# Gated cross-attention and a routed feed-forward layer: two weight loads, one share and two TensorE products placed elsewhere

## The reference

```python
x = x + tanh(g_xattn) * attention(layernorm(x), ctx, Wq, Wk, Wv, Wo)
x = x + tanh(g_ffn)   * ffn(layernorm(x), gate_w, gate_up_proj, down_proj)
```

```python
probs = softmax(x @ gate_w.T); w, idx = top_k(probs, 2); w = w / sum(w)
for each expert e:            # I = 1024
    g, u = split(x @ gate_up_proj[e].T)
    acc += combine[:, e] * (silu(g) * u @ down_proj[e].T)
```

## Time and profile before

| what | value |
|---|---|
| time, median of 3 runs | 438.24 us (438.04 to 438.81) |
| time of the profiled execution | 438.3 us |
| its span, first to last instruction | 436.5 us |
| mean granted TensorE clock | 0.969 of full |
| busy: TensorE, VectorE, ScalarE, GpSimd | 400.1, 213.2, 207.7, 255.1 us |
| chain that ended last | TensorE 75%, DMA 7%, GpSimd 5%, VectorE 4%, ScalarE 3%, issue 3% |

### The profile page before, as it was taken

One profiled execution on the slowest core, in us unless ns is written; L12 is line 12 of the kernel. 1 busy time (PEld: TensorE's weight loads), 2 busy tenths in 40 slices (PEclk: granted clock), 3 DMA queues, 4 the chain that ended last, 5 costly groups with the idle time before them and its releaser, 6 DMA issues.

```text
span 436.5 us, 10544 instructions
## 1 busy us (share of the span) xinstructions
PE 400.1 (92%) x2483; PEld 336.3 (77%) x2484; DVE 213.2 (49%) x582; ACT 207.7 (48%) x456; POOL 255.1 (58%) x251
## 2 busy tenths in 40 slices
PE   6979688899899999999999999999999999999960
PEld 6646446567788889888888988888888888888850
DVE  2556888789344544433443443454444344444430
ACT  1569876546633374356347332742356336432310
POOL 3105677794596389539728952595339827953221
PEclk9998889799999999999999999999999999999995
DMA  8970024504455325424612552164124621112211
GB/s 271 403 285 25 26 84 145 188 26 126 134 139 202 49 36 206 130 40 131 206 25 43 198 133 37 25 202 135 25 29 121 202 59 25 25 25 38 38 31 15
DMA packets 19629, 46.71 MB, mean 107 GB/s; under 512 B 2368, under 2 KB 13760, under 8 KB 16512
## 3 DMA queue, kind: packets, MB, share of 16 engines
q1 hardware_dynamic: 11632, 35.18, 23.4%
q0 software_dynamic: 6720, 9.64, 12.3%
q10 hardware_dynamic: 1248, 1.57, 1.0%
HBM read 37.64 MB, written 9.00 MB: 107 GB/s over the span
## 4 chain that ended last, share of the span: by engine, by line
PE 75%; DMA 7%; POOL 5%; DVE 4%; ACT 3%; issue 3%; SPq 0%; POOLq 0%; DVEq 0%; ACTq 0%
PE att L1073 21%; PE sc L1051 20%; PE misc L1051 10%; PE qbank L1051 10%; PE pT L1061 6%; DMA rows_scratch<-x 2%; DMA x<-in_x 2%; POOL dn L491 2%; ACT gu L678 2%; PE att L997 2%; PE att L843 1%; DMA out<-xT_all,index_out 1%; PE qbank L863 1%; PE sc L876 1%; POOL dn L422 1%
## 5 line engine op out<-in xcount | busy, mean ns | idle before, releaser
L567 POOL DMA_INDIRECT out<-xT_all,index_out x34 | 54.5, 1603 | 105.7 <-DVE xT_all L1363 97.1
L1073 PE MATMUL att<-dn,hT 128*128 x816 | 113.8, 289 | 1.5 <-DVE xT_all L1363 1.5
L1073 PEld LDWEIGHTS att<-dn,hT 128*128 128x128 f32 x816 | 101.6, 190 | 1.7 <-issue 1.7
L1051 PE MATMUL sc<-gu,xT 128*128 x408 | 102.1, 399 | 0.0
L1051 PEld LDWEIGHTS sc<-gu,xT 128*128 128x128 f32 x408 | 74.2, 188 | 14.6
L1051 PE MATMUL misc<-gu,xT 128*128 x204 | 80.5, 395 | 2.0 <-issue 1.1
L1051 PE MATMUL qbank<-gu,xT 128*128 x204 | 80.1, 393 | 0.0
L416 POOL TENSOR_TENSOR gu<-wraw,gu 128x2048 f32 (+1 forms) x14 | 64.5, 4626 | 1.6 <-issue 1.5
L1340 DVE TENSOR_TENSOR xT_all<-xT_all,sc 128x512 f32<-128x512 f32 x34 | 23.4, 689 | 83.2 <-ACT xT_all L762 83.2
L762 ACT ACTIVATE xT_all<-misc 128x512 f32<-128x512 f32 x34 | 20.3, 597 | 71.8 <-PE qbank L1051 71.7
L1340 DVE TENSOR_TENSOR xT_all<-xT_all,qbank 128x512 f32<-128x512 f32 x34 | 23.4, 688 | 59.5 <-ACT xT_all L762 59.5
(11 more groups left out here) (202 smaller groups left out, 472.7 us busy)
## 6 DMA issues: line engine op xcount, KB each, us to landing
wraw<-in_gu SPq DMA_DIRECT2D x16, 1024.0 KB, 5.4
wraw<-in_dn SPq DMA_DIRECT2D x8, 1024.0 KB, 5.1
x<-in_x SPq DMA_DIRECT2D x8, 266.0 KB, 12.3
xT_all<-in_xT SPq DMA_DIRECT2D x4, 512.0 KB, 11.6
out<-x SPq DMA_DIRECT2D x8, 256.0 KB, 2.6
rows_scratch<-x SPq DMA_DIRECT2D x3, 532.0 KB, 3.6
xT_all<-rows_scratch,index_in POOLq DMA_INDIRECT x36, 2.9
out<-xT_all,index_out POOLq DMA_INDIRECT x34, 3.9
```

Source lines behind the costliest of these rows:

```text
L567: nc.gpsimd.indirect_dma_start(out=out_d, out_offset=bass.IndirectOffsetOnAxis(ap=index, axis=0), in_=y[:, r, :], in_offset=None, compute_ ...
L1051: mm = nc.tensor.matmul(bank[2 * hf + n][:, :], xT[:, par, xp, k, :], gu_part(where, wp, k * 2 * I + col, HALF), start=(k == 0 and xp == 0 ...
L1073: mm = nc.tensor.matmul(bank[6][:, 0:D], hT[:, hf, hp, j * P:(j + 1) * P], dn_part(where, wp, (hf * JH + j) * D, D), start=(hf == 0 and j ...
```

## The change

Three parts of the hand-written order change; no computation is added to or taken from the result.

1. Pieces 3 and 4 (expert 1's gate and up weights) were loaded in batch 3's and batch 4's turn of the sync queue; both are now loaded in batch 2's, behind that batch's store of `x`. GpSimd raises `w_lo` by 2 in its turn 2 instead of turn 4.
2. On GpSimd, `share_out` of set 2 (batches 4 and 5) stands ahead of `mark_places` of batch 5 and of `last_rstds`, where it stood behind them.
3. On TensorE, turn 7 has two products more, of 512 and of 384 columns, whose results nobody reads: one ahead of `ranks`, one behind the second half of the transposed probabilities. Both wait for `lead_ready`.

```diff
@@ sync engine, loop over b
                 sp.dma_start(out_v[:, TB * b:TB * b + TB, :], x[:, TB * b:TB * b + TB, 0:D]).then_inc(out_init, 16)
-                if 3 <= b <= 4:
-                    load_piece(b)
+                if b == 2:
+                    load_piece(3)
+                    load_piece(4)
@@ GpSimd, loop over t
                 if t == B - 1:
                     place_values(NS - 3)
                     mark_places(B - 4)
+                    share_out(NS - 3)
                     mark_places(B - 3, 0, PICKS // 2)
                     last_rstds()
                     mark_places(B - 3, PICKS // 2)
-                    share_out(NS - 3)
                     share_out(NS - 2)
...
-                if t == 4:
+                if t == 2:
                     pool.wait_ge(w_lo_first, 2 * (PIECE // CHUNK))
                     pool.sem_inc(w_lo, 2)
@@ TensorE
+            def stay_warm(n):
+                pe.wait_ge(lead_ready, 1)
+                nc.tensor.matmul(qbank[:, 0:n], ident, const[:, 0:n], start=True, stop=True)
...
                 if t + 1 < B:
                     scores(t + 1)
+                if t == B - 1:
+                    stay_warm(512)
                 if t < B and t - 2 in ENDS:
                     ranks(ENDS[t - 2])
...
                     transpose_probs(t, 1)
+                if t == B - 1:
+                    stay_warm(384)
```

## The result

| | median | runs |
|---|---|---|
| after | 441.01 us | 4, 440.0 to 441.4 |
| before, same chip | 438.14 us | 4, 437.81 to 438.81 |

The ratio is 1.006, with a 95% interval of 1.0031 to 1.0089: the change makes the kernel 0.6% slower, where 436.3 us was forecast and 437.9 was the upper end. The profiled execution of after took 440.0 us (span 438.2), 1.7 us more than that of before.

The account below looks back on a forecast made before the run. TensorE bounds the block loop, so block 2's start decides: 1.6 us earlier, cut to 1.15 at `h_low(0, 0)`, plus 0.84 us of wait removed, makes 2.0 us, 438.3 to 436.3 us; own range 435.4 to 437.1, widened to 437.9 with rivals.

Parts of the forecast that it names:

- The lead store and the first gather: Sync queue and GpSimd: store lands in 3.6 us instead of 5.98, gather moves to 81.3, 1.6 us earlier.
- The two products: TensorE, turn 7: 0.97 and 0.72 us, covered to within 0.1 us if the clock stays full.
- The clock falls anyway, at the old place: Rival, TensorE after 81.6: second product costs 1.43 us at half clock; 438.7 us, chance 0.11.
- VectorE is then the later one: VectorE, batches 6 and 7: without its wait done at 86.55, block 0's first product 1.6 us earlier.
- TensorE, VectorE and GpSimd all stand 1.6 us earlier: Ahead of block 0: all three engines shift 1.6 us, block 0's first product from 90.05 to 88.45.
- get in each other's way less: VectorE and GpSimd: less mutual hindrance, a reason for the range's lower side, down to 435.4 us.
- The later fall of the clock: Rival, TensorE's stand from about 86.1: half clock 6.8 us, block 2 0.7 later; 439.0 us, chance 0.09.
- GpSimd becomes the bound: Rival: GpSimd's chain stays, the moved share adds 0.62 us, `last_rstds` ends at 98.9; 437.6 us, chance 0.18.
- The share: GpSimd, set 2: 0.62 us ahead of `last_rstds`; earlier row store removes TensorE's 0.84 us wait for block 2's rows.
- The price of the change: Block 2's first product: from 113.13 to 111.15, 2.0 us earlier, giving 436.3 us.

Follow-up runs that it names:

- e2: The kernel before with part 1 alone, weight pieces 3 and 4 loaded in batch 2's turn: 440.11 us, ratio 1.0056.
- e1: The kernel after, with GpSimd waiting for VectorE's slots of batches 4 and 5 before its last three low parts: 437.07 us, ratio 0.9983.
- e9: The kernel after without GpSimd's last three low parts, a plain ScalarE copy in their place (wrong numbers): 435.07 us, ratio 0.9906.
- f1: The kernel after with ScalarE's plain copy for the three low parts and three GpSimd memsets in their place: 439.77 us, ratio 1.0040.
- e4: The kernel before with part 2 alone, set 2's share ahead of batch 5's marks: 437.95 us, ratio 1.0000.
- the hold: Added to the kernel after: GpSimd waits for slots of batches 4 and 5 before its last three low parts; 0.9983 with the products, 0.9977 without.
- VectorE's low parts: The kernel after with the three low parts made by VectorE instead of GpSimd: 436.15 us, 0.9948; without the two products 436.30 us, 0.9958.
- e11: The kernel after without the two products and without GpSimd's three low parts, ScalarE's plain copy in their place: 435.76 us, ratio 0.9931.
- e3: The kernel before with part 3 alone, the two long products: 439.35 us, ratio 1.0042.
- e8: The kernel after with GpSimd's wait for the slots, but pieces 3 and 4 loaded at their old place: 438.74 us, ratio 0.9997.
- e6: The kernel after, with the three low parts waiting until VectorE's slot marks of batches 4 and 5 are done: 439.67 us, ratio 1.0024.
- e5: The kernel after, with GpSimd waiting for each low part's end before starting the next: 440.28 us, ratio 1.0029.

## Why the prediction was wrong, point by point

**The lead store and the first gather: right.** The store's 532 KB landed in 3.4 us (forecast 3.6), the gather stood at 80.97, 1.04 behind the tokens (forecast 81.3 and 1.02). Of the 1.6 us, GpSimd got 1.9.

**The two products: right in themselves.** They took about 0.96 and 0.7 us, both covered, and the clock stayed full from 80 to 90. The rival "The clock falls anyway, at the old place" is out.

**The step that failed** is "VectorE is then the later one. It had no work left at 86.21 - 0.72 = 85.49 … without the wait it is done at 86.55", and what follows from it, "TensorE, VectorE and GpSimd all stand 1.6 us earlier". I moved VectorE's and GpSimd's work by the same amount as if each were alone; where it names their collision at all, it has them "get in each other's way less", on the lower side of the range. But the parts of the change moved them by different amounts: VectorE's `slots` stayed where it was, from the tokens on, and GpSimd's gather and low parts moved 1.9 to 2.2 us towards it. The AND met them at their start and grew from 0.17 to 4.06 us; VectorE was done at 89.79, 3.2 later than forecast. That the loads alone do it is shown by e2, and that GpSimd's work in this place is what does it by e1, e9 and f1. The trace of before had the signs, and I didn't price them: VectorE's step `ties` at 88.44 took 1.06 us where the same step takes 0.18 in after, and ended with GpSimd's low parts.

**The later fall of the clock** was on record at 9%, with 439.0 us. It came, and in the place named, TensorE's stand ahead of batch 7's attention; but it isn't what cost the time. The rival had a stand of 0.9 us, half clock for 6.8 us and block 2 0.7 us later. Measured were a stand of 4.45 us, half clock for 3.4 us (90.1 to 93.5) and block 2 1.75 us later. Block 0 was to start at 88.45 and started at 91.81, and 3.2 of these 3.4 us are the late normalisation. The slow products cost TensorE some 0.7 us more up to 94.2, and nothing of that is left at block 2, which is as late against before as block 0 was. That 439.0 lay nearer to the result than the forecast is luck.

**"GpSimd becomes the bound"** fell in this form: GpSimd's chain was earlier, not later. It was its company that cost.

**The share: half right.** Block 2's gather no longer waits for the row stores but for the tokens; TensorE still waited 0.56 us for the rows, which were 4.66 us under way where I had taken 3.0. Alone the share is worth nothing that the times show (e4). GpSimd's last shares weren't done at about 100.6: the first of the two began at 101.73, after GpSimd had stood for 3.16 us (the profile names no releaser; ScalarE made their `odds` from 101.11), and the second was done at 103.49.

**The price of the change: mis-sized.** With the collision gone the change is worth 435.07 against 435.89, and 436.15 against 437.02: 0.8 and 0.9 us, not the 2.0 of the forecast (the intervals of the two ratios overlap in each pair, so the size is rough). And the products, on which half of the argument rested, give nothing that the times show clearly: 0.9983 with and 0.9977 without them under the hold, 0.9948 and 0.9958 with VectorE's low parts. Only e9 against e11 has 0.7 us, within the 0.5 to 1.5 expected if they are worth something, and there too the intervals overlap.

**What stays open.** The profiled execution of after lost 1.7 us, the medians 2.9; the other executions had no profile. That a run of three low parts holds one VectorE instruction for all three isn't explained. In e3, e4 and e8 too one step waited past the end of at least one low part, up to the end of the last. But in before's turn 4 a run of four, from 43.43 to 48.38, delayed three steps by 0.5 to 0.7 us each and let them go in between, and in e6 the same run of three (84.66 to 88.40) let VectorE in behind its second. And e6's ratio is 0.4% above e1's, while its stretch from the tokens to block 2 is only 0.4 us longer; I have no cause for that.

## What to carry to other kernels

When an edit moves one engine earlier, lay its new timeline beside those of the others instruction by instruction; in this kernel VectorE and GpSimd couldn't be moved past each other for nothing, and an instruction of 0.17 us took 4. Look in the trace of before for instructions whose longest is many times their median (289 and 1056 ns for the line of `ties` at 88.44): if such a one ends with an instruction of another engine, it may be a collision that the kernel already pays for. A stand that holds two engines back may be what keeps two others out of each other's way, so price the removal of a wait with its neighbours' work, not alone.

## What the runs showed of the hardware that I had not expected

A VectorE instruction on 128x8 integers waited for GpSimd for up to 3.9 us. The wait ended with the last of three low parts made back to back (87.27 and 87.23), and with pauses between them after the first (1.62 us in e5). The instruction's recorded start was 0.26 us ahead of the run's, while GpSimd issued a gather; in before the same instruction took 0.17 us during a gather alone. The wait was as long behind memsets (3.85 us in f1) as behind subtractions. Two-input steps of VectorE waited behind the subtractions as well (3.59 us in e3, 3.39 for the two of e5), and GpSimd's own run grew by 1.0 us in e1. Reductions didn't: one at 86.02 in e6, in the middle of a low part, took 0.17.

The Trainium skill, "SBUF — State Buffer", section "Who interferes with whom", says that VectorE and GpSimd share one pair of ports with an exclusive lock, that a `tensor_scalar` or a copy in a two-port mode contends for it, that an instruction with two inputs in the scratchpad contends with GpSimd's reads of it, that reductions don't, and that the loser fully blocks, for the other's whole instruction. The traces agree that the AND, behind memsets too, and the two-input steps waited, and the reduction didn't; in which mode the AND ran, no row shows. On how long, they show more than the page says: in after the wait spanned three instructions of GpSimd (0.17 to 4.06 us), not one.

The time of before ran from 436.0 to 440.6 us in 32 runs on one chip, with mean granted clocks of 0.965 to 0.983, and the slower runs had the lower clock on the whole (correlation -0.68). In the profiles the half-clock stretches lie at other places from run to run: in before from 50.8 to 57.3 and from 81.6 to 88.4 us, in e4, the same program up to there, from 63.3 to 66.8 and from 80.5 to 83.7. That these places make the whole spread of 4 us isn't shown. With 12 runs a kernel the intervals are still 0.2 to 0.3% to either side.
